# Second layer of a two-layer graph network: the MLP's first product in a bank of its own, and one gathered tile in two of three supertiles on TensorE

## The reference, cut to what matters

```
h = relu(layernorm(x));  x = x + segment_sum(h[src] * edge_weight[:, None], dst)
h = relu(layernorm(x))
w = (relu(edge_attr_32 @ W1 + b1) @ W2 + b2).reshape(e, 4, 8, 8)   # 32 -> 64 -> 256 per edge
s_e, v_e = s[src], v[src]                                           # gathered rows of h
m0 = 0.25 * (einsum(s_e * sh0, w_000) + C110 * einsum(v_e, sh1, w_110))
m1 = 0.25 * (einsum(s_e, sh1, w_011) + einsum(v_e * sh0, w_101))
x = x + segment_sum([m0, m1], dst) + self_interaction(h)
```

## Time and profile before

| | |
|---|---|
| median of 3 runs | 9337.08 us (9321.34 to 9354.07) |
| profiled execution | 9330.14 us, its span 9328.3 us |
| granted TensorE clock, mean | 0.856 of full speed |
| busy: PE, DVE, POOL, ACT | 79%, 58%, 52%, 33% |

### The profile page before, as it was taken

How to read it: one execution, slowest core, us unless ns; L and a number is a source line. 1 busy time by engine, 2 the same in 40 slices (tenths; PEclk the granted TensorE clock), 3 DMA queues, 4 the chain that set the end, 5 groups by cost and what they waited for, 6 DMA issues and landing times.

```text
span 9328.3 us, 170251 instructions
## 1 busy us (share of the span) xinstructions
PE 7326.0 (79%) x46802; PEld 4946.4 (53%) x46802; DVE 5420.8 (58%) x12253; ACT 3091.8 (33%) x13298; POOL 4880.8 (52%) x5215
## 2 busy tenths in 40 slices
PE   6888888888888886777777777777777777777777
PEld 5777777676777775444444444444444444444444
DVE  6666666666666665555555555555555555555555
ACT  2222222222222222433433343333333433333334
POOL 4666656666666665444444444444444444444444
PEclk9999999999999997788888888888888888888887
DMA  3111111111111111111111111111111111111111
GB/s 81 25 26 25 26 25 26 25 26 25 26 26 26 25 25 26 28 22 23 22 22 23 23 23 22 21 22 22 22 22 23 22 23 22 22 23 22 22 23 23
DMA packets 376870, 235.14 MB, mean 25 GB/s; under 512 B 114825, under 2 KB 373209, under 8 KB 376333
## 3 DMA queue, kind: packets, MB, share of 16 engines
q0 software_dynamic: 163424, 84.00, 6.9%
q1 hardware_dynamic: 212428, 147.61, 6.2%
q10 hardware_dynamic: 990, 3.21, 0.1%
HBM read 229.19 MB, written 5.23 MB: 25 GB/s over the span
## 4 chain that ended last, share of the span: by engine, by line
PE 30%; another core or an unknown queue 26%; issue 18%; DVE 18%; DVEq 5%; ACT 2%; DMA 0%; ACTq 0%; POOL 0%; POOLq 0%; SPq 0%
PE w_ps L696 22%; DVE prod L1174 4%; DVEq L993 3%; DVE t L1179 2%; PE w_ps L706 2%; PE hp_ps L824 2%; PE w_ps L777 2%; DVE z L1211 1%; DVE reduced_sb L1142 1%; DVE acc L1000 1%; DVE reduced_sb L1139 1%; DVE prod L1183 1%; DVE vsh L1158 1%; DVE pick L1010 1%
## 5 line engine op out<-in xcount | busy, mean ns | idle before, releaser
L446 POOL DMA_INDIRECT z<-h_table,idx x5107 | 4836.7, 947 | 4359.1 <-DVE prod L1183 2015.2
L696 PE MATMUL w_ps<-parts,pick 128*128 128x448 f32 x11662 | 2766.0, 390 | 355.2 <-issue 284.1
L696 PEld LDWEIGHTS w_ps<-parts,pick 128*128 128x128 f32 x11662 | 2284.4, 201 | 635.7 <-issue 422.0
L548 ACT ACTIVATE z<-z,squares 128x32 f32<-128x32 f32 x3125 | 798.4, 311 | 2758.1 <-issue 2511.8
L824 PE MATMUL hp_ps<-parts,pick 128*128 128x448 f32 x4340 | 1190.6, 413 | 50.7 <-issue 48.6
L1164 DVE TENSOR_TENSOR p<-w_ps,scalars 128x320 f32<-128x320 f32 x625 | 302.9, 485 | 1498.9 <-remote 1486.7
L824 PEld LDWEIGHTS hp_ps<-parts,pick 128*128 128x128 f32 x4340 | 857.8, 211 | 283.5 <-issue 224.1
L599 ACT ACTIVATE hid<-w_ps,b_sb 128x320 f32<-128x320 f32 x625 | 329.6, 527 | 1946.0 <-remote 1702.7
L777 PE MATMUL w_ps<-w_sb,hid 64*128 64x256 f32 x5000 | 929.9, 497 | 5.2 <-issue 4.3
L1010 DVE TENSOR_TENSOR pick<-sc_ps,feat 128x896 fp32r<-128x896 f32 x833 | 889.7, 1089 | 52.6 <-issue 44.6
L793 PE MATMUL sc_ps<-prod,onehot 128*32 128x344 f32 x5000 | 672.1, 475 | 300.1 <-issue 168.1
(11 more groups left out here) (96 smaller groups left out, 6429.1 us busy)
## 6 DMA issues: line engine op xcount, KB each, us to landing
z<-h_table,idx POOLq DMA_INDIRECT x5107
feat<-key_table SPq DMA_DIRECT2D x311, 192.0 KB
ft_sh_sb<-in_ft_sh SPq DMA_DIRECT2D x625, 90.0 KB
feat<-key_table SPq DMA_DIRECT2D x210, 64.0 KB
h_table<-big SPq DMA_DIRECT2D x10, 280.0 KB
rel_sb<-in_dst_t SPq DMA_DIRECT2D x1, 1562.5 KB
idx_all<-in_src_t SPq DMA_DIRECT2D x1, 1532.5 KB
squares<-in_ew_t SPq DMA_DIRECT2D x1, 1532.5 KB, 12.5
```

What stands on the lines that cost most here:

```text
L446: pool.indirect_dma_start(z[:, r, u, :], None, rows, bass.IndirectOffsetOnAxis(ap=idx[:, r, u:u + 1], axis=0)).then_inc(z_in[r], 16)
L548: last = nc.scalar.activation(z[:, r, u, :], z[:, r, u, :], ACT.Copy, scale=ew_all[:, bass.ds(n * G + u, 1)])
L696: mm = pe.matmul(fold_ps[:, pick_banks[k], 0:NC * D], pick[:, k, blk, :], parts[:, t, :, blk, :], start=(blk == 0 and t == 0), stop=(blk = ...
```

## The change

- `on_pe(r)` becomes r % 3 > 0: in two of three supertiles TensorE gathers one tile, so GpSimd issues 5, 4, 4 gathers instead of 4, 5. TensorE does it in parts: 14 matmuls in the iteration with r % 3 = 0, then 6, then 8. A ring of six has four such tiles (`PAIRS1`), with four slots of keys and picks.
- VectorE makes the pick of every second of these tiles. ScalarE makes the others (`make_pick1`): seven Abs of 128 elements and one Relu of 896, after its own one-hot rows in the iteration with r % 3 = 1.
- `hidden` writes to a bank of its own and is issued one supertile ahead. It is no longer two matmuls on 64 rows each but two on all 128 rows, with a w1 that is half zeros. ScalarE's relu is one ahead too.
- The weights of the first four tiles stay double-buffered, two banks each. The fifth tile's weights have one bank, not double-buffered, shared with the folded sums (`total1_ps`). TensorE fills it last (`last_weights`), after VectorE has freed it (`last_wts_used`), and then sends `wts_ready`.
- VectorE's three products are therefore six: three on the last tile first, then three on the first four tiles, then `select_group1`.
- SyncE loads keys as two DMAs of two rows for each ring, where one of three rows stood, and waits for both makers of picks.
- `st_inv` shares its space with `st_neg`.

```diff
     def on_pe(r):
-        return r % 2 == 0
+        return r % PERIOD > 0
...
+        last_wts_ps = w_ps[:, 0, 2, 0:WN].rearrange("p (e c) -> p e c", c=4 * MUL)
-        total1_ps = [w_ps[0:D, q, 2, 384:384 + WIN] for q in range(2)]
+        total1_ps = w_ps[0:D, 0, 2, 384:384 + WIN]
-        hidden_ps = [w_ps[:, q, 1:3, 0:HALF // 2] for q in range(2)]
+        hidden_ps = w_ps[:, 1, 2, 0:HALF].rearrange("p (h e) -> p h e", h=2)
...  SyncE
-                        sp.wait_ge(pick1_ready, nth(b, r) + 1)
-                        load_keys1(first, count)
+                        sp.wait_ge(pick1_ready, b * (PAIRS1 // 2))
+                        sp.wait_ge(pick1_by_act, b * (PAIRS1 // 2))
+                        load_keys1(first, most)
...  ScalarE
+                for blk in range(GB):
+                    last = nc.scalar.activation(far[:, blk], key1[:, slot1(r, e)], ACT.Abs, scale=-1.0, bias=rows_sb[:, blk:blk + 1])
+                last.then_inc(pick1_far, 1)
+                nc.scalar.activation(pick[:, slot1(r, e)], far, ACT.Relu, scale=-1.0, bias=one_sb[:]).then_inc(pick1_by_act, 1)
-                    act.wait_ge(hidpre_ready, n + 1)
-                        act.wait_ge(wts_ready, n - 1)
-                    relu_hidden(r % 2).then_inc(hid_ready, 1)
+                    act.wait_ge(hidpre_ready, n + 2)
+                        act.wait_ge(wts_ready, n)
+                    relu_hidden((r + 1) % 2).then_inc(hid_ready, 1)
...  TensorE, one iteration
-                    pe.wait_ge(wts_used, n - 1)
-                    hidden(r, q).then_inc(hidpre_ready, 1)
-                    half_gather()
-                    edge_sums()
-                    pe.wait_ge(hid_ready, n + 1)
-                    total = fold_sums(q, q)
-                    weights(q).then_inc(wts_ready, 1)
+                    pe.wait_ge(hid_ready, n + 1)
+                    hidden((r + 1) % R1).then_inc(hidpre_ready, 1)
+                    gather_part()
+                    pe.wait_ge(wts_used, n - 1)
+                    weights(q)
+                    edge_sums()
+                    pe.wait_ge(last_wts_used, n)
+                    total = fold_sums(q)
+                    last_weights(q).then_inc(wts_ready, 1)
...  VectorE, after wts_ready
-                select()
+                scalar_products(last_wts_ps, last_tile)
+                dve.wait_ge(coef_ready, n + 1)
+                vector_rows(last_wts_ps, last_tile)
+                take()
+                step(2)
+                scalar_rows(last_wts_ps, last_tile).then_inc(last_wts_used, 1)
+                scalar_products(wts_ps[q], first_tiles).then_inc(prod_step, 1)
+                vector_rows(wts_ps[q], first_tiles)
+                scalar_rows(wts_ps[q], first_tiles).then_inc(wts_used, 1)
+                select()
```

More of the change, by code:

```diff
@@ L139, in gnn_two_layers @@
         st_sum, st_neg, st_var = (sb(n, [NP, J]) for n in ("st_sum", "st_neg", "st_var"))
-        st_std, st_inv = (sb(n, [NP, J]) for n in ("st_std", "st_inv"))
+        st_std, st_inv = sb("st_std", [NP, J]), st_neg
         st_eps = st_var
@@ L598, in relu_hidden @@
             def relu_hidden(q):
-                return nc.scalar.activation(hid[:, q].rearrange("p (h e) -> p h e", h=2), hidden_ps[q], ACT.Relu, bias=b1_sb[:])
+                return nc.scalar.activation(hid[:, q].rearrange("p (h e) -> p h e", h=2), hidden_ps, ACT.Relu, bias=b1_sb[:])
             def scale_rows(n, r, q, selection=lambda: None):
@@ L608, in scale_rows, with make_pick1 @@
                 last.then_inc(coef_ready, 1)
+            def make_pick1(b, r, s):
+                base, e = 0 if s is None else s - r, PERIOD - 1
+                if s is not None and s + e + R1 >= S:
+                    return
+                loads = R1 // PERIOD if s is None else sum(base + R1 + p * PERIOD + 1 < S for p in range(R1 // PERIOD))
+                act.wait_ge(keys1_in, b * (16 * R1 // PERIOD) + 16 * loads)
+                if s is None or s >= R1:
+                    act.wait_ge(picked1, nth(b, r, e) + 1)
+                for blk in range(GB):
+                    last = nc.scalar.activation(far[:, blk], key1[:, slot1(r, e)], ACT.Abs, scale=-1.0, bias=rows_sb[:, blk:blk + 1])
+                last.then_inc(pick1_far, 1)
+                act.wait_ge(pick1_far, b * (R1 // PERIOD) + r // PERIOD + 1)
+                nc.scalar.activation(pick[:, slot1(r, e)], far, ACT.Relu, scale=-1.0, bias=one_sb[:]).then_inc(pick1_by_act, 1)
             def edge_rows(b, r, s):
@@ L653, in edge_rows @@
                 nc.scalar.activation(onehot[:, v], near[:], ACT.Relu, scale=-1.0, bias=one_sb[:]).then_inc(hot1_ready, 1)
+                if r % PERIOD == 1:
+                    make_pick1(b, r - 1, None if s is None else s - 1)
                 if s == 1:
@@ L761, in _, with hidden @@
             self_interaction(GR - 1, GU - 1)
-            def hidden(r, q):
+            def hidden(r):
                 for h in range(2):
-                    rows = slice(h * HID, (h + 1) * HID)
-                    mm = pe.matmul(hidden_ps[q][:, h], w1_sb[rows, :], ft_sb[rows, r, :], start=True, stop=True)
+                    mm = pe.matmul(hidden_ps[:, h], w1_sb[:, h], ft_sb[:, r, :], start=True, stop=True)
                 return mm
             def weights(q):
-                for k, cols in enumerate((2 * WN, 2 * WN, WN)):
+                for k in range(2):
                     rows = slice(32 * k, 32 * k + 3)
-                    pe.matmul(w_ps[:, q, k, 0:cols], ones_sb[rows, :], b2_rows[rows, 0:cols], start=True, stop=False)
+                    pe.matmul(w_ps[:, q, k, :], ones_sb[rows, :], b2_rows[rows, :], start=True, stop=False)
                 for j in range(2):
@@ L868, in wide_weights @@
                 pe.nop(nofuse=True)
-                hidden(0, 0).then_inc(hidpre_ready, 1)
+                hidden(0).then_inc(hidpre_ready, 1)
                 pe.wait_ge(hid_ready, n + S + 1)
                 pe.nop(nofuse=True)
-                weights(0).then_inc(wts_ready, 1)
+                weights(0)
+                last_weights(0).then_inc(wts_ready, 1)
             def wide_sums1(turn):
```

175 lines of the change are left out of this document (108 added, 67 removed).

## The result

The changed kernel takes 9000.92 us (median of 4 runs, 8962.16 to 9006.39), the kernel before on the same chip 9345.58 us (4 runs, 9321.34 to 9365.66). The ratio is 0.9623, 95% interval 0.9587 to 0.966. The profiled execution took 9005.56 us, its span 9003.8. The forecast was 9228: the sign was right and the time lies in the range, but the gain is 345 us where the sum had 109.

What follows compares the result with a forecast made beforehand. It took the second layer to be bound by waits on TensorE signals held during GpSimd's gather runs. Terms −131 + 125 + 23 − 230 + 104 + 0 = −109 us on 9330 gave 9221, forecast 9228 us; range 8800 to 9620.

Steps and rivals of the forecast that it cites:

- What bounds the kernel, and the hold: Second layer: no engine is full; TensorE's signals are held up while GpSimd's gather runs last beyond some three.
- rival A: Second layer: the weights' signal gets out before the long gather run delays it; −600 us on top, about 8630; chance 0.20.
- Gathers, −131: GpSimd, second layer: 13 gathers instead of 13.5 in three supertiles, half a gather saved each cycle; −131 us.
- Products, picks and selections, +125 and +23: VectorE, second layer: six product instructions for three, +125 us; fewer picks but more selections, +23 us.
- L1204, −230: VectorE's wait in front of the selection, second layer: two thirds of its 343.2 us won back, −230 us.
- ScalarE's pick, +104: ScalarE, second layer: up to 3.9 us of pick a cycle, mostly covered; 0.5 us a cycle counted, +104 us.
- rival C: ScalarE, second layer: its pick always falls in the free part, half uncovered; +400 instead of +104, 9520; chance 0.10.
- TensorE, 0: TensorE, second layer: seven more matmuls a cycle and an unpaired hidden product lie beside VectorE's work; 0 us.
- rival B: Second layer: TensorE's records, some 97 ns each, set the pace; +283 us, 9620; chance 0.15.

Runs made afterwards that it cites:

- b_pause_2: Kernel before, with GpSimd waiting for its own 1024-column memset ahead of each second-layer supertile's first and third gather: 9044.76 us, ratio 0.9847.
- b_weights_first_3: Kernel before, with only TensorE's weights moved ahead of the window sums, on a chip with held signals: 8938.12 us, ratio 0.973.
- a_third: Changed kernel, but TensorE gathers one tile in only one of three supertiles and ScalarE makes no picks: 8915.15 us, ratio 0.9705.

## Why the prediction came out as it did

- **What bounds the kernel, and the hold.** Right, and now shown by a change to GpSimd's program alone (`b_pause_2`). That a hold needs a run "beyond some three" gathers was too coarse: with runs of two or three, waits of 2.2 us remain.
- **The step that failed** is that the sum kept the cycle of three supertiles with its run of nine gathers and its wait of 8 us, priced edits inside that cycle, and gave the move of the weights ahead of the window sums nothing. The missing term is the −249 us of `b_weights_first_3`, in which nothing else is changed. I had put this move only into rival A, at 0.20, and against A stood one row: a signal 2.4 us into the long run did not get out. I asked whether the signal passes within that cycle, and not what the cycle becomes when VectorE has the weights already and waits for the sums instead, which it needs 3.9 us after its first product (6015.31 to 6019.20): it then mostly frees no slot early enough in a run to lengthen it, and the runs of nine fall from 187 to 49.
- **Rival A** shows the sign that I gave for it: "remote" in front of the first product fell by 1198 us. The move is also worth nearly half of its −600. But its mechanism is not what the traces show: in `b_weights_first_3` the signal leaves as late in the run as before, and in the changed kernel one sent 1.9 us into a run (6017.52, run from 6015.65) is still held. That the time lies in the range is partly luck: half of A was kept in it for a reason that did not hold.
- **The rest of the sum.** All the other parts together come to some −22 us (−271 less −249, on two chips), where the sum had −109.
- **Gathers, −131.** Not seen: `a_third` is as fast with one gather more in three supertiles, though it has less other work, so the term alone was not measured.
- **Products, picks and selections, +125 and +23.** VectorE's busy time rose by 252 us over the layer, inside the 100 to 300 that I gave. L1227 takes 349 ns for 192 elements and 948 for 768, the price I read from before.
- **L1204, −230.** The wait lost 327 us, more than taken; but it is hardly a gain of its own. With the selection where it was, `b_weights_first_3` stands 27.6 us there, so that wait too came from the order. The late selection alone gives 0.3% on a free chip; on a holding one it was not run.
- **ScalarE's pick, +104; rival C.** Its price was right (7 × 0.386 + 1.042 = 3.7 us against 3.9), its cover better: VectorE waits 25.9 us for `scalars` and 6.3 for `coef`. What I did not cost is the other side: all picks on VectorE would take 177 us more.
- **TensorE, 0; rival B.** Here right: the layer made 60210 records in 5240 us, 11.5 a microsecond and not 10.3, so no fixed price for each record is the pace. But "TensorE is idle in every hold" was wrong: it had 10 records from 6018 to 6024. B's 9620 was also not B's sum: it is the median before plus 283, while −109 + 230 + 283 = +404 would give some 9740. On free chips TensorE is the bound, and the change costs 92 us.

## What to carry to other kernels

Where a wait is named "remote", look at what another engine does from the recorded end of the work to the start of the waiter: here a run of gathers was the price, and not GpSimd's load, which the pauses raised. On a chip that shows such waits, break the run with a short pause before rebuilding the order of the other engines, and look which signal an engine meets first inside a run, and whether it can lengthen the run from there. Measure on more than one chip: the same change was 3.8% and 2.9% faster on holding ones and 1.4% slower on a free one.

## What the hardware showed that I had not expected

- One kernel takes 6545 and 6550 us on two chips, 9187 to 9193 on three and 9346 in the run of the result. The first layer shows it too: with its code unaltered, GpSimd's gathers of the second begin at 2959 to 2965 us on free chips and at 3624 to 3682 on holding ones. Why only some chips hold the signals stays open.
- Two pauses in each supertile, 0.58 us each, make the kernel before 11.6% faster on a holding chip. Two of 1.41 us each make it 1.5% faster there, and 27.9% slower on a free chip.
- In the long run of gathers TensorE's own instructions nearly stop: 10 records from 6018 to 6024 us, after 41 in the six microseconds before. In the same six VectorE and ScalarE have none.
- The Trainium skill, "SBUF — State Buffer", section "Who interferes with whom", says PE and ACT never wait on anyone. The wait for TensorE's signals during GpSimd's gathers, some 10 us in the earlier trace rows, is outside that rule on holding chips, though nothing here says that it is one for an SBUF port; on free chips nothing speaks against the rule.
